# A decoder block on one core: beta diagonals by ScalarE, decay tables from PSUM by VectorE, weight rounding taken from GpSimd

## The reference

```python
qkv = x @ W_qkv.T;  z = x @ W_z.T
beta = sigmoid(x @ W_b.T);  decay = exp(-softplus(x @ W_a.T + dt_bias) * exp(A_log))
q, kk, v = split(depthwise_conv4(qkv));  kk = kk / norm(kk)
def step(state, inp):                       # for each token, head and value head
    Sk = k_t @ state
    state = state * d_t + k_t (x) (v_t - Sk) * b_t
    o = q_t @ state
out = rmsnorm(o, norm_w) * silu(z);  y = out @ W_out.T
x = x + attn(ln(x));  x = x + cross_attention(ln(x), ctx);  x = x + ffn(ln(x))
```

## Time and profile before

| what | value |
|---|---|
| median of three runs | 4518.85 us |
| profiled execution, its own time | 4521.22 us |
| span of the profiled core | 4519.4 us |
| mean granted TensorE clock | 0.962 |
| PE / DVE / ACT / POOL busy | 88% / 70% / 50% / 42% |
| PE / DVE / ACT / POOL busy, 1300 to 1600 us | 281.29 / 254.56 / 178.93 / 158.97 of 300 us |
| granted TensorE clock, 1300 to 1600 us | 1.00 |
| delta_net, first projection to last output add | 92.7 to 3120.8 us |

### The profile page before, as it was taken

The page is one execution under the profiler, slowest core; times in us unless marked ns, Lnnn a source line. Parts: engine busy times, 40 slices in busy tenths (PEclk is TensorE's granted clock), DMA queues, the critical chain, the costliest instruction groups (busy, mean ns, idle before and its releaser), DMA issues. The chain is left out here.

```text
span 4519.4 us, 75144 instructions
## 1 busy us (share of the span) xinstructions
PE 3998.6 (88%) x26288; PEld 2920.6 (65%) x26288; DVE 3161.6 (70%) x5082; ACT 2237.8 (50%) x4061; POOL 1898.3 (42%) x1852
## 2 busy tenths in 40 slices
PE   3899999999999999999999999995788989389998
PEld 2677777777776777767777777774344444178887
DVE  3788888888888888888888888884556556632222
ACT  1465655556565655656565565653344445221111
POOL 1365554545455554545455454543233333311110
PEclk8899999999999999999999999997799999699999
DMA  2001010101001011010101010101565563000001
GB/s 74 15 29 36 25 36 21 41 25 32 29 20 41 24 32 30 29 32 24 32 30 36 25 36 21 29 27 31 94 91 90 83 92 60 38 24 19 19 14 38
DMA packets 134066, 172.39 MB, mean 38 GB/s; under 512 B 12524, under 2 KB 79980, under 8 KB 133132
## 3 DMA queue, kind: packets, MB, share of 16 engines
q1 hardware_dynamic: 131212, 166.03, 15.9%
q10 hardware_dynamic: 2432, 1.05, 0.2%
HBM read 143.12 MB, written 21.76 MB: 36 GB/s over the span
## 5 line engine op out<-in xcount | busy, mean ns | idle before, releaser
L405 PE MATMUL pj<-xh,w_hi 128*128 128x512 f32 x1536 | 686.1, 447 | 26.3 <-ACT conv_k L612 17.8
L990 POOL TENSOR_TENSOR silu_z<-silu_z,exp_z 128x512 f32<-128x512 f32 x128 | 184.6, 1442 | 1216.9 <-ACT exp_z L629 1216.9
L405 PE MATMUL pj<-xh,w_lo 128*128 128x512 f32 x1536 | 608.0, 396 | 0.0
L405 PE MATMUL pj<-xl,w_hi 128*128 128x512 f32 x1536 | 603.3, 393 | 0.0
L1518 DVE TENSOR_REDUCE row_max<-s 128x1 f32<-128x512 f32 x512 | 341.9, 686 | 271.8 <-PE s L1272 268.6
L975 POOL TENSOR_SCALAR b_t<-qk_masked,beta_section 128x256 f32<-128x256 f32 (+1 forms) x512 | 490.5, 968 | 21.5 <-ACT qk_masked L714 20.2
L1452 ACT ACTIVATE probs<-s 128x512 f32<-128x512 f32 x512 | 291.3, 595 | 325.0 <-PE s L1296 319.4
L756 DVE SCALAR_TENSOR_TENSOR conv_v<-conv_in,conv_w_section,conv_v 128x512 f32<-128x512 f32 x384 | 403.7, 1051 | 20.2 <-ACT conv_v L612 9.1
L680 ACT ACTIVATE kk_masked<-tp 128x512 f16<-128x512 f32 x320 | 191.5, 598 | 323.7 <-PE tp L496 320.2
L405 PEld LDWEIGHTS pj<-xh,w_hi 128*128 128x128 f32 x1536 | 291.8, 190 | 83.3 <-issue 31.2
L405 PEld LDWEIGHTS pj<-xh,w_lo 128*128 128x128 f32 x1536 | 289.6, 189 | 67.4
(11 more groups left out here) (259 smaller groups left out, 10250.9 us busy)
## 6 DMA issues: line engine op xcount, KB each, us to landing
w_raw<-in_w_in SPq DMA_DIRECT2D x128, 256.0 KB, 3.5
decays<-decay_by_head SPq DMA_DIRECT2D x64, 512.0 KB, 3.8
decays<-decay_by_head SPq DMA_DIRECT2D x64, 256.0 KB, 4.9
q_stack<-qk_parts SPq DMA_DIRECT2D x128, 128.0 KB
k_stack<-qk_parts SPq DMA_DIRECT2D x128, 128.0 KB
f_raw<-in_f_w SPq DMA_DIRECT2D x32, 256.0 KB, 2.7
x_all<-in_x SPq DMA_DIRECT2D x4, 1024.0 KB, 11.5
source<-in_ctx SPq DMA_DIRECT2D x8, 512.0 KB
```

Of the source, the lines that this page charges most:

```text
L405: mm = pe.matmul(pj[j % 2][:, :], a[:, j, k * P:(k + 1) * P], b[:, k, bp * WIN:(bp + 1) * WIN], start=(n == 0), stop=(n == 3 * KT - 1))
```

## The change

Seven things change in `delta_net`.

- The added table of the decay scan is no longer a constant identity but beta on the diagonal (`beta_diag`), which ScalarE writes with eight small copies of the identity scaled by beta (`act_beta`). The scanned tables then hold beta already, and the constant `scan_diag` is gone.
- VectorE multiplies the scanned tables straight with the products in PSUM, both value heads in one instruction (`dve_table`): four instructions for a_t in place of eight, and four for b_t, which GpSimd did in sixteen. ScalarE's copies of the products (`act_kq`) are gone. a_t is made at the end of the section before, b_t after the first u.
- The masked evictions of levels 5 and 6 go from VectorE to ScalarE (`act_x`), which copies only the rows and columns that the mask keeps: two pieces a block at level 5, one at level 6.
- The low part of the gated output goes to VectorE, behind the evictions of levels 2 and 3.
- Weights are rounded by ScalarE and their remainders taken by VectorE, in sections 0, 1 and 2 of a head, and the ring has four buffers.
- On TensorE the key products of the next section come before the second d0p, and the two z half projections behind it move one place later. The norms use tp and ms1 as banks.
- GpSimd keeps the SiLU product alone.

```diff
-RING = 2
+RING = 4
-            dve.tensor_tensor_scan(dec[:, i, :], dec[:, i, :], diag, 0.0, ALU.mult, ALU.add)...
+            dve.tensor_tensor_scan(dec[:, i, :], dec[:, i, :], beta_diag[:, i, :], 0.0, ALU.mult, ALU.add)...
+        def dve_table(dve, t, b, c, out, kq, done, after):
+            E["kq"].wait(dve, t, kq)
+            E["dec"].wait(dve, t, b * PV + PV - 1)
+            sl = (slice(0, SEQ), slice(SEQ, TRI))[c]
+            o = c + after
+            dve.tensor_tensor(out[:, b * PV:(b + 1) * PV, sl], dec[:, b:NM:2, sl.start + o:sl.stop + o],
+                              kq_bank[kq][:, sl].unsqueeze(1).to_broadcast([P, PV, sl.stop - sl.start]), ALU.mult)\
+               .then_inc(E[done].sem, 1)
+        def act_x(act, s, lv, c):
+            E["xp"].wait(act, s, 2 * (lv - 1) + c)
+            b = 1 << lv
+            for n in range(P // (2 * b)):
+                rows = slice(2 * b * n + b, 2 * b * (n + 1))
+                act.activation(by_mat(x_l[c][lv - 1][rows, :])[:, :, 2 * b * n:2 * b * n + b],
+                               xp[c][rows, 0:H].rearrange("p (m n i) -> p m n i", m=NM, i=b)[:, :, n, :], ACT.Copy)\
+                   .then_inc(E["xa"].sem, 1)
+        def act_beta(act, t, q):
...
+            for c in range(2):
+                o = c * (SEQ + 1) + 1
+                act.activation(beta_diag[:, slot(q), o:o + P], ident, ACT.Copy,
+                               scale=beta_s[:, 2 * (q // PV) + c, q % PV:q % PV + 1]).then_inc(E["bd"].sem, 1)
+        def act_weights(act, hk_w, j):
+            w_loaded[j % RING].wait(act, hk_w, 16 * (j // RING) + 15)
+            act.activation(piece(j)[0], w_raw[:, j % RING, :], ACT.Copy).then_inc(w_rounded.sem, 1)
+        def dve_weights(dve, hk_w, j):
+            w_rounded.wait(dve, hk_w, j)
+            hi, lo = piece(j)
+            dve.tensor_tensor(lo, w_raw[:, j % RING, :], hi.bitcast(F32), ALU.subtract).then_inc(w_split.sem, 1)
...
-            gates(nc, xh, xl, a["w_ab"], gate_const, cols, beta, decay_rows)
+            with nc.cleanup_on_exit():
+                gates(nc, xh, xl, a["w_ab"], gate_const, cols, beta, decay_rows)
```

More of the change, by code:

```diff
@@ L443, in pe_out_norms @@
             if more:
-                E["km"].wait(pe, s + 1, 3)
-            pe.matmul(ms[p][:, :], ones, osq[p][:, :], start=True, stop=True).then_inc(E["oss"].sem, 1)
+                E["at"].wait(pe, s + 1, 3)
+            pe.matmul(sum_bank[p][:, :], ones, osq[p][:, :], start=True, stop=True).then_inc(E["oss"].sem, 1)
         def pe_y(pe, s, hk, i, bank_read):
@@ L467, in pe_first @@
             E["u0"].wait(pe, s, c)
-            if c == 0 and after_out:
-                E["delta"].wait(pe, s + -1, 1)
-            elif after_out:
-                E["oln"].wait(pe, s + -1, 1)
+            if after_out:
+                E["oln"].wait(pe, s + -1, c)
             for q in range(NM):
@@ L508, in pe_group, with pe_section @@
             mm.then_inc(E[event].sem, 1)
-        def pe_section(pe, s, bp, hk, prev, nxt):
+        def pe_section(pe, s, bp, hk, prev, nxt, first, more):
             def proj(j, half):
@@ L564, in pe_section @@
                 pe_kq(pe, s + 1, 1)
+            E["rhs1r"].wait(pe, s, 0)
+            pe_group(pe, xp[0], lambda q: u_f[:, 1, mat(q)], v_r, "d0p")
+            proj(GATE + 1, 0)
+            E["d0"].wait(pe, s, 1)
+            pe_group(pe, xp[1], lambda q: a_t[:, q, SEQ:TRI], d0[:, :].bitcast(F32), "rp")
+            proj(GATE + 1, 1)
             E["res"].wait(pe, s, 1)
@@ L692, in act_section @@
                     act.activation(v_r[:, :], v_t[:, 0, :], ACT.Copy).then_inc(E["vr"].sem, 1)
+                    if bp == 2 and more:
+                        for j in (VALUE, VALUE + 1):
+                            E["pj"].wait(act, s + 1, j)
+                            act_weights(act, hk + 1, j)
+                    if bp == 0 and not first:
+                        for j in (GATE, GATE + 1):
+                            E["pz"].wait(act, s + -1, j - GATE)
+                            act_weights(act, hk, j)
+                if lv == 3 and bp == 2 and more:
+                    for j in (KEY, QUERY):
+                        E["pj"].wait(act, s + 1, j)
+                        act_weights(act, hk + 1, j)
+                if lv == 1 and bp == 1 and not first:
+                    E["y"].wait(act, s + -2, 3)
+                    for j in (CHUNKS, CHUNKS + 1):
+                        act_weights(act, hk, j)
                 if lv == 5 and nxt:
@@ L853, in dve_section @@
                        .then_inc(E["xm"].sem, 1)
+                if lv in (2, 3) and prev:
+                    dve_gated_rest(dve, s + -1, lv - 2)
+                if lv in (2, 3) and bp == 1 and not first:
+                    dve_weights(dve, hk, CHUNKS + lv - 2)
                 if lv == 4 and prev:
@@ L857, in dve_section @@
                     dve_conv(dve, t, lv - 1)
+                if lv == 4 and bp == 2 and more:
+                    dve_weights(dve, hk + 1, KEY)
+                    dve_weights(dve, hk + 1, QUERY)
                 if lv == 5 and prev:
                     dve_y(dve, s + -1, prev[1], 2)
+                if lv == 5 and bp == 0 and not first:
+                    dve_weights(dve, hk, GATE)
+                    dve_weights(dve, hk, GATE + 1)
+                if lv == 5 and bp == 2 and more:
+                    dve_weights(dve, hk + 1, VALUE)
+                    dve_weights(dve, hk + 1, VALUE + 1)
             dve_rest(dve, s, 0)
@@ L883, in dve_section @@
                 dve_decays(dve, t, 3)
-            E["dp2"].wait(dve, s, 1)
-            dve.tensor_tensor(delta[1], tp[:, :], d0[:, :].bitcast(F32), ALU.add).then_inc(E["delta"].sem, 1)
+                dve_a(dve, t, 1, 0)
+                dve_a(dve, t, 1, 1)
         def dve_prologue(dve):
@@ L891, in dve_prologue @@
             dve_conv_weights(dve, first, 0)
+            dve_beta(dve, first, 0, 0)
+            for j in range(RING):
+                dve_weights(dve, 0, j)
             for j in range(GATE):
                 dve_conv(dve, first, j)
+            for j in range(RING, PIECES):
+                dve_weights(dve, 0, j)
             dve_norm_guard(dve, first)
@@ L897, in dve_prologue @@
                 dve_decays(dve, first, q)
+            for b in range(2):
+                for c in range(2):
+                    dve_a(dve, first, b, c)
         def dve_epilogue(dve, s, hk):
             dve_gated(dve, s)
+            for p in range(PV):
+                dve_gated_rest(dve, s, p)
             for i in range(4):
@@ L910, in head @@
                     nxt = (hk, bp + 1) if bp < NSEC - 1 else None if last else (hk + 1, 0)
-                    section(eng, Section(hk, bp), bp, hk, prev, nxt)
+                    section(eng, Section(hk, bp), bp, hk, prev, nxt, first, not last)
             prologue(eng)
```

191 lines of the change are left out of this document (82 added, 109 removed).

## The result

| | before | after |
|---|---|---|
| median, us (4 runs each on this chip) | 4520.0 (4514.2 to 4521.9) | 4339.0 (4338.1 to 4339.5) |
| ratio of the two | | 0.9601, 95% interval [0.9585, 0.9618] |
| span of the profiled execution | 4519.4 | 4337.5 |
| TensorE busy, 1300 to 1600 us | 281.3 | 289.4 |
| VectorE, ScalarE, GpSimd busy there | 254.6, 178.9, 159.0 | 246.7, 212.0, 20.1 |

The change wins 181 us. 123 were forecast, with a range that ended at 4355; the sign was right, the size 57 us short and outside the range. The granted clock is 1.00 in that stretch in both kernels, so the sections can be compared as they are.

The account below looks back on a forecast made before the run. TensorE was taken to bound the loop, so only its waits could go: 1.7 us over 64 sections, 109 us, plus 14 outside, took 4521.2 to 4398 us (4396 on the median's scale); range 4375 to 4420, 4355 to 4450 with A and B.

Parts of the forecast that it names:

- first u, evictions, short waits, low part (quiet): TensorE's waits before level 6: 0.40 for u, 1.21 falling to 0.1, 0.4 short, 0.12 low part.
- levels 5 and 6 by ScalarE: Evictions: level 5's four pieces fit under a half product; level 6's wait falls from 1.04 to 0.6, winning 0.44 us.
- TensorE's order: Behind cp, key products of 1.3 us replace a 1.48 us half projection; second d0p waits 0.2 us more.
- weights: Roundings on ScalarE and remainders on VectorE in sections 0 to 2 cost 2.5 us a head, 0.63 a section.
- prologue, with section 0 (13), and epilogue (1): Before the loop, copies and projections start earlier, 13 us; after it, two GpSimd products become VectorE's, 1 us.
- First u: Section start: shorter a_t tables bring u 2.7 us earlier, so TensorE's wait of 0.40 us goes.
- Evictions: Before `pe_tu`: faster convolutions without GpSimd's b_t cut waits from 1.21 to 0.1 us, short waits by 0.4.
- A: VectorE relieved by more: slow convolutions of sections 0 and 2 vanish, weight waits halve; 4364 us, chance 0.16.
- B: GpSimd's SiLU beside i_minus_a holds VectorE, u is late; 0.7 us a section, 4441 us, chance 0.23.
- C: VectorE becomes the bound in levels 2 to 5, convolutions stay slow; 4588 us, chance 0.06.
- D: Nothing won in the loop, waits move to u_final and adds, only prologue stays; 4507 to 4515, chance 0.05.
- signs of being wrong: TensorE's loop matmuls no longer the longest line, or TensorE waiting for ScalarE, not VectorE, outside level 6.

Follow-up runs that it names:

- e12: Kernel before with all of GpSimd's loop work but SiLU (b_t, low part, weight splits) on one column; 4374.9 us, ratio 0.9686.
- e14: Kernel before with GpSimd's loop work but SiLU on one column and evictions of levels 5 and 6 by ScalarE; 4303.5 us, ratio 0.9528.
- e1: Kernel after with the evictions of levels 5 and 6 back on VectorE; 4419.9 us, ratio 0.9782.
- e6: Kernel before with only the evictions of levels 5 and 6 moved to ScalarE, in pieces; 4459.5 us, ratio 0.9863.
- e5: Kernel after with the loop's weights split by GpSimd again, four buffers kept; 4386.6 us, ratio 0.9701.
- e11: Kernel after with GpSimd's SiLU products on one column instead of 512; 4338.1 us, ratio 0.9606.
- e8: Kernel after with the weights' roundings and remainders moved to idle places and two heads a loop turn; 4309.8 us, ratio 0.9533.
- e10: Kernel after with weights' instructions in idle places, next head's first loads before section 3's decays, and all fourteen heads written out; 4272.5 us, ratio 0.9457.
- e4: Kernel before with GpSimd's sixteen b_t instructions on one column each; 4504.6 us, ratio 0.9965.

## Why the prediction was wrong

Per section of the loop, in us:

| step of the prediction | forecast | measured | by |
|---|---|---|---|
| first u, evictions, short waits, low part (quiet) | 2.08 | 2.24 | e12 |
| levels 5 and 6 by ScalarE | 0.44 | 1.16 | e12 to e14; 1.1 by e1, 0.95 by e6 |
| TensorE's order | -0.20 | -0.11 | tail, e14 to after |
| weights | -0.63 | -0.67 | e14 to after |
| sum | 1.69 | 2.62 | |
| prologue, with section 0 (13), and epilogue (1) | 14 | 15.8 | trace after; all of it up to the first output product |

**The step that failed is "Levels 5 and 6".** It priced level 6 at 0.44, and that was near (0.51). To level 5 it gave nothing but the finding that four pieces fit into the cover. There the wait was 0.4 to 0.5 us in the kernel before, and 1.1 in section 2 (4.09 to 4.21 and 4.78 us against 3.69), and it was counted within's first line, which the paragraph on evictions let fall to 0.1 as the convolutions got faster. That paragraph walked VectorE through levels 1 to 4 (0.7 + 2.3 + 0.6 against 3.75) and stopped there. At level 5 an add to x_all stands ahead of the eviction as well, and e12 shows the piece at 4.21 us beside a quiet GpSimd: contention was not its cause, but for 0.57 us in section 2 (4.78 to 4.21). Moving the evictions gave 0.55 at level 5, 0.51 at level 6 and 0.1 in section 0's tail, where VectorE is no longer behind. This is 0.72 of the 0.93 us a section that were missing, 46 of 57 us.

**First u.** The wait went, as said, but not by the reason given. I had credited the shorter a_t; e12 keeps the old a_t and gets the same 5.90 us. What went was GpSimd's b_t beside a_t, i_minus_a and u. In section 0 nothing was won (6.99 against 6.89), though e12 has 6.52 there and e14 6.60 with the same branch. Why the kernel after has 0.4 us more than these stays open.

**Evictions.** Right in size, not in place, and so right by luck. 1.63 us a section were forecast for levels 1 to 5 (1.11 of visible waits, 0.4 of short ones, 0.12 of the low part). e12 measures 1.53 in levels 1 to 4 and 0.06 in level 5. The waits too short for the list were thus more than the 0.4 I gave them, and made up for level 5: two errors of the term that cancelled. The walk gave 3.6 against 3.75 us a level, and the levels stand at 3.65 to 3.69.

**Weights.** 0.63 forecast, 0.67 measured: 1.45, 0.84 and 0.40 in sections 1, 2 and 0, against 1.1, 1.1 and 0.3. e5 shows that leaving them on GpSimd would have cost 48 us more.

**Rivals.** A had the size nearest (4364), for a part of the reason: section 0's and 2's slow convolutions did go whole, but the weight waits were not halved. B's mechanism is real and hidden (e11). C did not come: convolutions are at 750 ns in every section. D is refuted by the sections.

**The checks** that the prediction named came out so: sections 42.6 to 45.6 us (44.0 to 45.2 said), section 1 and not 2 the longest without a branch, three convolution instructions at 2.3 us, no wait for the first u, level 6's wait by ScalarE at 0.35 us and 0.17 hidden, i_minus_a at 126.7 us. The first of them was already too high because of level 5. One of its signs of being wrong did come: outside level 6's evictions TensorE waits for ScalarE, 24.7 us for u_final and 5.0 for level 5's second block, and for VectorE's evictions only 3.5 us. For u_final this was in the prediction's own terms, which let that wait stay; for level 5 it was not.

How much of e8's and e10's gains is the branch and how much the shifted start of code stays open: e1 shows that the same branch can cost ScalarE 1.0 us more when the code around it changes, and I did not try to move it alone.

## What to carry to other kernels

When a wait is explained by contention, walk every level that it is summed over: one row of the list of waits held two causes here, and only one was cured. Taking work off a second engine pays little when what is left of it slides into the next critical place; e4 took GpSimd's busy time from 159 to 102 of 300 us and won 15 us, e12 took it to 72 and won 143. An instruction moved to an idle place can outrun its own DMA, so its load is to be moved with it, and then what stands behind that load in the queue.
